# Edge keys by broadcast transfers, in a graph attention layer with a quantised feed-forward block

## The reference

```python
def _L0_gnn_ref(x, edge_index, edge_type, edge_type_weights, wq, ..., wo, bo):
    q = x @ wq.T + bq; k = x @ wk.T + bk; v = x @ wv.T + bv
    q2 = (q @ wiq.T + biq).reshape(N, H, D).transpose(1, 0, 2)   # k2, v2 likewise
    w = softplus(edge_type_weights)
    mask = full((N, N), -inf).at[src, dst].set(w[edge_type - 1])
    # the diagonal gets w[3] where no edge set it
    scores = einsum('hnd,hmd->hnm', q2, k2) / 8 + mask[None]
    out = einsum('hnm,hmd->hnd', softmax(scores), v2)
    return out.transpose(1, 0, 2).reshape(N, OUT_F) @ wo.T + bo

x = x + _L0_gnn_ref(_layernorm(x), stack([src, dst]), edge_type_5, ...)
x = x + _L0_ffn_ref(_layernorm(x), ...)   # gate, up, down with weights and activations rounded to 8 bits
```

## Time and profile before

| | |
|---|---|
| median of 3 runs | 336.85 us (335.77 to 340.67) |
| profiled execution | 334.56 us |
| its span, first to last instruction | 332.7 us |
| TensorE busy | 322.2 us (97%), clock 0.998 |
| VectorE, ScalarE, GpSimd busy | 68%, 55%, 56% |

### The profile page before, as it was taken

The page is one execution under the profiler, slowest core; times in us unless marked ns, Lnnn a source line. Parts: engine busy times, 40 slices in busy tenths (PEclk is TensorE's granted clock), DMA queues, the critical chain, the costliest instruction groups (busy, mean ns, idle before and its releaser), DMA issues.

```text
span 332.7 us, 5989 instructions
## 1 busy us (share of the span) xinstructions
PE 322.2 (97%) x2086; PEld 297.1 (89%) x2086; DVE 225.6 (68%) x600; ACT 182.3 (55%) x333; POOL 187.0 (56%) x253
## 2 busy tenths in 40 slices
PE   4999999999999999999999999999999999999994
PEld 4899998878999999999999999999999877887864
DVE  3857898856255556554185977879797875497574
ACT  4847257464333333333375968668595865243562
POOL 5686668547777766789816484563726757000000
PEclk9999999999999999999999999999999999999999
DMA  7997335667234333493411240302213110000005
GB/s 257 367 406 283 126 129 167 215 195 236 65 122 129 128 122 126 127 338 113 141 65 66 68 149 36 128 21 108 70 57 128 64 66 0 0 2 0 2 0 191
DMA packets 16763, 41.71 MB, mean 125 GB/s; under 512 B 3440, under 2 KB 7392, under 8 KB 16736
## 3 DMA queue, kind: packets, MB, share of 16 engines
q1 hardware_dynamic: 13824, 38.87, 34.1%
q0 software_dynamic: 2064, 1.80, 1.8%
q10 hardware_dynamic: 848, 0.70, 0.6%
HBM read 37.99 MB, written 3.37 MB: 124 GB/s over the span
## 4 chain that ended last, share of the span: by engine, by line
PE 90%; DVE 4%; DMA 2%; ACT 1%; POOL 1%; issue 1%; SPq 0%; DVEq 0%; ACTq 0%
PE PS L756 65%; PE PS L913 5%; PE PS L901 5%; PE PS L889 4%; PE PS L1048 2%; PE PS L737 1%; DMA V<-in_w_down 1%; DMA X<-in_x 1%; PE PS L1102 1%; PE PS L825 1%; PE PS L815 1%; PE PS L747 1%; PE PS L800 1%; PE PS L819 1%; POOL QT L460 1%; PE PS L790 1%
## 5 line engine op out<-in xcount | busy, mean ns | idle before, releaser
L422 POOL TENSOR_TENSOR ring<-stage,ring 128x256 fp32r<-128x256 f32 x124 | 90.3, 765 | 39.3 <-ACT ring L507 36.7
L756 PE MATMUL PS<-XT,ring 128*128 128x384 f32 x528 | 93.3, 335 | 0.0
L756 PEld LDWEIGHTS PS<-XT,ring 128*128 128x128 f32 x528 | 91.4, 188 | 0.1
L440 POOL DMA_INDIRECT codes<-ecol,place x51 | 60.3, 1182 | 26.4 <-issue 14.2
L507 ACT ACTIVATE ring<-stage 128x1024 fp32r<-128x1024 f32 x52 | 54.3, 1057 | 6.2 <-DMA stage<-in_weights 2.3
L614 ACT ACTIVATE scratch<-scratch,smx 128x384 f32<-128x384 f32 x48 | 28.9, 604 | 18.5 <-DVE smx L1345 18.5
L756 PE MATMUL PS<-QT,ring 128*128 128x384 f32 x192 | 35.5, 338 | 0.0
L756 PE MATMUL PS<-AT,ring 128*128 128x384 f32 x192 | 35.2, 338 | 0.0
L756 PEld LDWEIGHTS PS<-AT,ring 128*128 128x128 f32 x192 | 33.0, 188 | 1.5 <-issue 1.5
L756 PE MATMUL PS<-ring,AT 128*128 128x512 f32 x144 | 34.1, 393 | 0.0
L1249 DVE TENSOR_TENSOR ring<-stage,ring 128x1024 fp32r<-128x1024 f32 x21 | 25.7, 1227 | 12.1 <-issue 8.4
(11 more groups left out here) (200 smaller groups left out, 466.5 us busy)
## 6 DMA issues: line engine op xcount, KB each, us to landing
stage<-in_weights SPq DMA_DIRECT2D x56, 512.0 KB
V<-in_w_gate_up SPq DMA_DIRECT2D x4, 512.0 KB, 7.6
codes<-scratch SPq DMA_DIRECT2D x3, 576.0 KB, 14.5
X<-in_x SPq DMA_DIRECT2D x3, 512.0 KB, 5.2
out<-X SPq DMA_DIRECT2D x4, 384.0 KB, 2.6
scratch<-codes POOLq DMA_DIRECT2D x2, 576.0 KB, 5.7
scratch<-in_w_gate_up SPq DMA_DIRECT2D x2, 512.0 KB
V<-in_w_down SPq DMA_DIRECT2D x5, 176.0 KB, 5.2
```

The costliest lines, as they stand in the source:

```text
L422: ins = pool.tensor_tensor(ring[1][:, slot, piece], stage[:, slot % STAGE, piece], ring[0][:, slot, piece].bitcast(F32), ALU.subtract)
L440: pool.indirect_dma_start(codes[b].rearrange("(n a) -> n a", a=1), bass.IndirectOffsetOnAxis(ap=place[:, t:t + 1], axis=0), ecol[:, VAL, t ...
L756: ins = pe.matmul(outs, lhs[a], rhs[b], start=start and n == 0, stop=stop and n == 2, skip_group_check=True)
```

## The change

GpSimd computes the key rows (src x 384 + dst, 56 x 128 float32) in SBUF and stores them in memory as `key_rows`. SyncE then loads them, broadcast to all 128 partitions, by five transfers (`load_keys`), four of 12 columns of edges (768 KB written) and one of 4. They land in `QT[0]`, `QT[1]` and `PT[0][1]`, which hold nothing yet. `once(g)` reads its row there, and no longer a PSUM bank. The key products on TensorE with their semaphores and `sel` are gone, and so is the wait for `key_used` in chunk 8. On VectorE the groups 2s - 2 and 2s - 1 are done in step s, where 2s and 2s + 1 were, and `place` in step 7. On SyncE the order of the early loads is new, and the three table fills stand behind chunk 7.

```diff
-        erow = sb("erow", [2 * EC, P], I32)
-        rows = sb("rows", [2 * EC, P], F16)
-        sel = sb("sel", [2 * EC, EC], F16)
+        erow = sb("erow", [EC, 2, P], I32)
+        rows = sb("rows", [EC, 2, P], F32)
...
-        KEYS = 4
+        KEY_PART = 3
+        key_area = [QT[0], QT[0], QT[1], QT[1], PT[0][1]]
+        key_cols = [area[:, :, :].rearrange("p k n -> p (k n)").bitcast(F32)[:, at_c:at_c + n * 4 * P]
+                    for area, at_c, n in zip(key_area, (0, 12 * P, 0, 12 * P, 0), (3, 3, 3, 3, 1))]
...
-            sp.wait_ge(blank_ready, 1)
-            for b in range(LISTS):
-                sp.dma_start(codes[b].rearrange("(m p n) -> p m n", m=NT, p=P), blank.to_broadcast([P, NT, N])
-                             ).then_inc(codes_blank[b], 16)
+            def load_keys(q):
+
+                sp.wait_ge(rows_out, 16)
+                at_q, n = q * KEY_PART * 4 * P, key_cols[q].shape[1]
+                sp.dma_start(key_cols[q], key_rows[at_q:at_q + n].rearrange("(a n) -> a n", a=1).to_broadcast([P, n])
+                             ).then_inc(key_in[q], 16)
+
+            def fill_tables():
+
+                sp.wait_ge(blank_ready, 1)
+                for b in range(LISTS):
+                    sp.dma_start(codes[b].rearrange("(m p n) -> p m n", m=NT, p=P), blank.to_broadcast([P, NT, N])
+                                 ).then_inc(codes_blank[b], 16)
...
+            load_keys(0)
             sp.wait_ge(t_full, KT)
             load_ffn(0, 0)
+            next_chunk(4)
+            load_keys(1)
+            next_chunk(5)
+            load_keys(2)
             load_ffn(1, 0)
-            next_chunk(4)
+            next_chunk(6)
+            load_keys(3)
+            load_keys(4)
+            next_chunk(7)
             load_ffn(2, 0)
-            next_chunk(5)
-            for c in range(6, 10):
+            fill_tables()
+            for c in range(8, 10):
                 next_chunk(c)
...
-            chain.step(pool.affine_select(out=sel[:, :], in_=sel[:, :], compare_op=ALU.not_equal, fill=float(N),
-                                          base=0, pattern=[[-1, EC]], channel_multiplier=1))
-            pool.affine_select(out=sel[:, :], in_=sel[:, :], compare_op=ALU.not_equal, fill=1.0,
-                               base=-EC, pattern=[[-1, EC]], channel_multiplier=1).then_inc(rows_ready, 1)
...
             pool.wait_ge(edges_in, 2 * 16)
-            pool.tensor_copy(rows[:, :], erow[:, :]).then_inc(rows_ready, 1)
+            chain.link(pool.tensor_scalar(rows[:, 0, :], erow[:, 0, :], float(N), None, ALU.mult))
+            chain.step(pool.tensor_copy(rows[:, 1, :], erow[:, 1, :]))
+            chain.step(pool.tensor_tensor(rows[:, 0, :], rows[:, 0, :], rows[:, 1, :], ALU.add))
+            pool.dma_start(key_rows.rearrange("(e p) -> e p", e=EC), rows[:, 0, :]).then_inc(rows_out, 16)
...
-                if s == 0:
-                    pe.wait_ge(rows_ready, 2)
-                for g in (2 * s, 2 * s + 1):
-                    if g < 13:
-                        keys(g)
...
-                    if c == 0 and m == 2:
-                        pe.wait_ge(key_used, 13)
...
-                dve.wait_ge(key_full, g + 1)
+                q = g // KEY_PART
+                dve.wait_ge(key_in[q], 16)
                 for n in range(4):
                     e = 4 * g + n
-                    ins = dve.scalar_tensor_tensor(later[:, g % 2 * 4 + n, :], PS[:, KEYS + g % 2, n * P:(n + 1) * P],
+                    at_e = (e - q * KEY_PART * 4) * P
+                    ins = dve.scalar_tensor_tensor(later[:, g % 2 * 4 + n, :], key_cols[q][:, at_e:at_e + P],
                                                    ecol[:, KEY, e:e + 1], tri[:, :], ALU.is_equal, ALU.mult,
                                                    accum_out=dup[:, e:e + 1])
...
-                for g in (2 * s, 2 * s + 1):
-                    if g < GROUPS:
+                for g in (2 * s - 2, 2 * s - 1):
+                    if 0 <= g < GROUPS:
                         once(g)
-                if s == 6:
+                if s == 7:
                     dve.wait_ge(key_used, GROUPS)
```

More of the change, by code:

```diff
@@ L62, in gnn_ffn @@
 def gnn_ffn(nc, x, weights, biases, bias_o, edge_cols, edge_rows, edge_w, clips,
-            w_gate_up, w_down, codes, out):
+            w_gate_up, w_down, codes, key_rows, out):
     with ExitStack() as ctx:
@@ L216, in gnn_ffn @@
         acc_free = sem("acc_free")
-        rows_ready = sem("rows_ready")
+        rows_out = sem("rows_out")
+        key_in = [sem(f"key_in{q}") for q in range(5)]
         cols_ready = sem("cols_ready")
@@ L225, in gnn_ffn @@
         pool_chain = sem("pool_chain")
-        key_full = sem("key_full")
         key_used = sem("key_used")
@@ L382, in _ @@
             pool.memset(turner[:, :], 0.0).then_inc(consts, 1)
-            pool.memset(sel[:, :], 0.0).then_inc(consts, 1)
-            pool.wait_ge(consts, 10)
+            pool.wait_ge(consts, 9)
             pool.affine_select(out=turner[:, :], in_=turner[:, :], compare_op=ALU.not_equal, fill=1.0,
@@ L492, in _ @@
             act.dma_start(edges[:, :, :], edge_cols).then_inc(edges_in, 16)
-            act.dma_start(erow[:, :], edge_rows).then_inc(edges_in, 16)
+            act.dma_start(erow[:, :, :], edge_rows.rearrange("(h e) p -> e h p", h=2)).then_inc(edges_in, 16)
             act.dma_start(bias[:, :], biases).then_inc(small_in, 16)
@@ L498, in _ @@
                           ).then_inc(small_in, 16)
-            act.wait_ge(consts, 11)
+            act.wait_ge(consts, 10)
             chain.step(act.activation(rs[:, 6, :], kinds[:, 0:NT], ACT.Sqrt))
@@ L731, in _ @@
             pe.sem_inc(w_used, RING)
-            pe.wait_ge(consts, 11)
+            pe.wait_ge(consts, 10)
             def keep_clock(n, columns=slice(0, N), bank=0):
@@ L792, in ffn_turn @@
                 ins.then_inc(ffn_full, 1)
-            def keys(g):
-                if g > 1:
-                    pe.wait_ge(key_used, g - 1)
-                for n in range(4):
-                    e = 4 * g + n
-                    ins = pe.matmul(PS[:, KEYS + g % 2, n * P:(n + 1) * P],
-                                    sel[:, e:e + 1].to_broadcast([2 * EC, P]), rows[:, :], start=True, stop=True,
-                                    skip_group_check=True)
-                ins.then_inc(key_full, 1)
             def low_last(s):
@@ L1243, in ffn_step @@
                                   ).then_inc(ffn_q, 1)
-            dve.wait_ge(consts, 11)
+            dve.wait_ge(consts, 10)
             dve.wait_ge(cols_ready, 1)
@@ L1589 @@
     codes = [nc.dram_tensor(f"codes{b}", (N * N,), F32, kind="Internal").ap() for b in range(LISTS)]
-    gnn_ffn(nc, *args, codes, out)
+    key_rows = nc.dram_tensor("key_rows", (EC * P,), F32, kind="Internal").ap()
+    gnn_ffn(nc, *args, codes, key_rows, out)
     result = run_bass_kernel_spmd(nc, [arrays], core_ids=[0])
```

## The result

The changed kernel takes 346.78 us (median of five runs, 342.02 to 348.41) against 336.85 us before. The ratio is 1.027, with a 95% interval of 1.020 to 1.035. In a second session the same kernel took 340.21 us against 335.56, ratio 1.015 (1.012 to 1.019). The change is a loss; the forecast was 343.2. The profiled execution took 342.02 us (span 339.9; before 334.56 and 332.7), 7.2 us more in the span. The two executions next to the median have spans of 344.6 and 344.7 us and a mean granted clock of 0.990 and 0.985, against 1.000 in the profiled one.

A forecast was written before the change was run, and what follows sets the result against it. TensorE, 97% busy, bounds the kernel, with VectorE's place, scatters and tables a second chain with 1.4 us to spare. Tables 6.9 (9.1) us late less 1.4 gave 5.5 (7.7), taken as 6.4: 336.85 + 6.4 = 343.2 us, range 335.5 to 347.

The forecast's parts named there:

- The contention: VectorE's `once` rows, now with two SBUF inputs, alternate with GpSimd's low-part pieces: 0.72 to 0.80 us a pair.
- The row that was said to be missing: No profile row shows `once` with two SBUF inputs beside GpSimd; its behaviour was taken from rows of the same kind.
- some 700 ns: Sign to look for: mean of the `once` line well over 345 ns, at this size, with its longest near 1 us.
- The forward working: Four queues worked through steps 0 to 7, with pairs of 0.72 (0.80) us: first scatter 8.1 (10.3) us late.
- The wait of the third feed-forward turn: After chunk 8, TensorE waits some 2.2 (2.5) us for the third feed-forward turn.
- The sum: Tables 6.9 (9.1) us later, chunk 31 with 1.4 us to spare: 5.5 (7.7) us net, taken as 6.4.
- the second chain: VectorE's `place`, then scatters, tables and `k_tile(5)` before chunk 31, beside TensorE with only 1.4 us to spare.
- TensorE's own 2.8 (5.1) us: TensorE's lateness by chunk 10 against the kernel before, with the 3.0 us gained from key products already in it.
- What was costed at nothing: GpSimd's key rows at the start, SyncE's store, key transfers and new load order: 0 us, hidden by idle time or slack.
- rival (c): Early transfers slower than 416 GB/s; 20% slower adds 1 to 3 us to whichever case holds; chance 0.08.
- (a): No contention: SBUF operands cost `once` nothing, first scatter 1.6 us later; 334.5 to 337 us, taken 336.3; chance 0.22.
- (b): Row and piece never overlap, 0.97 us a pair; TensorE waits over 5 us before step 5; 345 to 348; chance 0.10.

The follow-up runs named there:

- written out: ScalarE's two loops over the Q and K projections unrolled, with constant waits: kernel before 334.60 us, ratio 1.0004; changed kernel 341.73 us, ratio 1.020.
- experiment 2: Changed kernel with `tri` copied once into a PSUM bank and read there by `once`: 334.06 us, ratio 0.995.
- experiment 5: Kernel of experiment 3, key products kept, with `once` reading `ident` from SBUF in place of the key bank: 342.34 us, ratio 1.020.
- experiment 1: The changed kernel again with no edit, for a second profile: 340.21 us, ratio 1.015.
- experiment 6: Kernel before plus the change's key rows, store, five broadcasts (read by nobody) and SyncE order; key products kept: 339.20 us, ratio 1.011.
- experiment 8: Kernel of experiment 2 with each `edges_over` one tile later: 341.73 us (332.62 to 345.83), too scattered for a ratio.
- experiment 7: Kernel of experiment 4 with the change's SyncE order, table fills behind chunk 7: 339.49 us, ratio 1.012.
- experiment 9: Changed kernel with each `edges_over` one tile later: 345.28 us, ratio 1.020.
- experiment 3: Kernel before with the scatters going to fixed distinct places that do not depend on `once`: 334.82 us, ratio 0.999.
- experiment 4: Kernel of experiment 3 without TensorE's key products, `once` waiting for nothing: 335.95 us, ratio 1.001.
- experiment 11: Changed kernel with ScalarE's two loops over the Q and K projections unrolled, waits on constants: 341.73 us, ratio 1.020.
- experiment 12: Changed kernel with `tri` in PSUM, edges one tile later, ScalarE's loops unrolled, groups dealt over steps 1 to 6: 334.01 us, ratio 0.998.

## Why the prediction was right, and where it was not

The measured 346.78 us lies in the range (335.5 to 347), 3.6 us above the forecast. The three measured differences, +9.9, +4.7 and, written out, +7.1 us over the kernel before, lie on both sides of the forecast +6.4.

**The contention** held in mechanism and in size. A pair of row and piece was put at 0.72 to 0.80 us and takes 0.745. The pattern worked out for step 1 (two rows pass, four pairs, two free rows) is the one on the timeline. The row that was said to be missing, `once` beside GpSimd, turned out like its neighbours. Its reach was over-sized: the prediction reckons with some twenty rows that meet a piece, and 13 do. So the sign "some 700 ns" for the mean of the line did not come (477 ns), and the longest row stayed at 848 ns. Experiments 2 and 5 show the contention from both sides. The Trainium skill, "SBUF — State Buffer", section "Who interferes with whom", says that a VectorE instruction with two SBUF inputs contends with a GpSimd instruction that reads SBUF, and that one with at most one SBUF input, outside its two-port modes, does not. 848 ns against 349 for the longest row agrees with both halves.

**The forward working** of the four queues came out as follows, forecast first: `tile_low(3)` 36.1 (36.4) us, 36.51; tile 5 47.3 (49.2), 47.59; tile 7 58.9 (61.1), 57.57; `place` done 60.9 (63.1), 59.51; TensorE's waits 1.4 (1.7), 0.3 (0.6), 2.0 (3.2) before steps 5 to 7, measured 1.84, 0.17, 1.63. Up to tile 5 it is good to half a microsecond at the low end. The eight rows of step 6 were forecast at 4.9 (5.2) us and took 2.4 (51.09 to 53.46 us): `edge_values` beside them cost a row at most 0.06 us, so everything behind came earlier than worked out. The wait of the third feed-forward turn, put at 2.2 to 2.5 us, measured 0.34: that term was over-sized. The first scatter was 7.25 us late, not 8.1.

**The sum.** The step that failed is the end of the second chain: that TensorE waits for `k_tile(5)` before chunk 31, and that this "is the later of the two chains, so TensorE's own 2.8 (5.1) us are inside it". In the profile of the changed kernel there is no such wait. TensorE's own lateness had reached 7.3 us by chunk 32 and the mask cost it nothing. The terms there are -3.0 for the keys, +4.7 for the five early waits and +3.4 for the waits after 90 us. This leaves 2.1 us to the 7.2 of the span. Of these 0.5 us stand ahead of the first weight product (13.83 us against 13.34), which came at 13.39 in experiment 1, so they are not the change's; the rest lies in no idle row. The waits after 90 us are ScalarE's late ones, which the prediction did not have at all.

Written out, where they are absent, TensorE does stand before chunk 31, for 2.48 us, but for low part 31. The prediction has no term for that one: it looks at low parts 32 and 33 and gives them 3 us in hand. Low part 31 begins at 148.95 us, 5.6 us later than before, and the copies of the edges then stretch it by 2.5. The chain up to the tile was over-sized: the first table is back 149.24 - 145.80 = 3.4 us late, not 6.9. The first scatter is 6.8 us late; the scatters give back 1.4 (59.9 to 145.0 us, against 53.1 to 139.65 before; 1.2 was forecast), and the way from the last scatter to the table another 1.9 (4.2 us against 6.15). By the profile that the prediction read, TensorE is 2.3 us late of itself (forecast 2.8) and chunk 31 starts 5.0 us late (forecast 5.5, taken at 6.4). The clock, which the prediction did not have, adds 1.7. So the number came out near by a wait of about the right size for another reason, and a clock loss that was missing: that 6.7 us in the spans and 7.1 in the medians are near 6.4 is partly luck.

In the changed kernel's own profile the scatters gave back 6.2 us: they were busy for 55.9 us, against 60.3, and waited 8.2 us for landings, against 12.2. Why is not shown.

**What was costed at nothing** cost nothing in the changed kernel's profile: the first low part starts at 12.52 us (12.49 before), with the keys and fills the transfers ran at 404 GB/s between 22 and 36 us, and TensorE waits for no load. The key transfers took 9.2 us from issue to landing under that load and none is waited for. So rival (c) does not show in the changed kernel; experiment 6, whose ratio is above 1.005, does not settle it by time.

**The rivals.** (a), no contention, is refuted for the change, but experiment 2 is its world: 0.995, with the first scatter 1.8 us late where it had said 1.6, and of the 3.0 us half is kept (334.06 against 335.56). The rest did not go to the wait for the mask that it named: in that profile TensorE stands 2.25 us for low part 31, and then the clock falls. (b), full strictness at 0.97 us a pair, is refuted by 0.745.

## What to carry to other kernels

Moving an operand from PSUM to SBUF is not neutral: count the SBUF inputs of a VectorE operation that runs beside GpSimd, and keep one in PSUM, if only a constant copied there once. Work taken off the busiest engine is worth nothing until what feeds it is early enough; here loads, low parts and the clock took back half or more of the 3.0 us. Where an engine waits for several things, work out from the code what it needs and when each was done: the name in the bracket is only the one that came last. An operation that has become late meets new neighbours; low part 31 ran free before the change and beside the copies after it. When two profiles of one kernel differ in where they lose, first find a form in which the disturbance is gone for both kernels, and compare those.

## What the runs showed of the hardware that I had not expected

**Waits on a register's value that end late.** In the loop `early` ScalarE sometimes went on 3 to 4 us after TensorE's result was there. The waits that the trace gave to "remote" summed to 23.4 us in the changed kernel's profile (six waits), 22.7 in experiment 8 (six), 12.5 in experiment 7 (three), 8.8 in experiment 9 (two), 6.3 in experiment 1 (one) and 3.5 in experiment 2 (one). There were none in the profiles of the kernel before and of experiments 3 to 6, and none in the three kernels with the loop written out. Written out, the kernel before was no faster (1.0004); in its own profile TensorE never stood for such a wait. Why a wait ends late is open: nothing tried tells the wait on a register from the loop's branch, and whether it happens more in the changed kernel than before is not shown either. All six profiles that have such waits put the table fills behind chunk 7, but so does experiment 6, which has none.
The Trainium skill, "Runtime: NRT & Kernel Launch", section "Instruction fetch mechanics", says that a taken branch whose target is not in the pages at hand stops the engine until they are fetched; no run here shows whether that happened in this loop.

**The clock after a wait.** TensorE's granted clock stayed at 1.00 behind an idle time of 1.83 to 1.84 us in three profiles (the first, experiments 1 and 11), and in a fourth (experiment 9) it fell to 0.50, 1.2 GHz, behind the same one. It also fell behind the idle times of 1.98 us (experiment 4), 2.25 (experiment 2), 2.48 (experiment 11) and 2.95 us (experiment 7). In experiments 4 and 11 the fall cost 1.7 us: so a wait of some two microseconds cost nearly four there.

**GpSimd beside VectorE's copies.** A piece of low part (128x256) takes 0.70 us alone and 1.95 to 2.04 us beside a `copy_predicated` of 128x1152 (experiments 2, 11 and 12), and the three waits of TensorE before chunk 31 in these profiles, 2.25, 2.48 and 0.88 us, each stand behind such pieces.
